# Weights of the third stage split by ScalarE and GpSimd and turned by DMA transposes; ScalarE makes the norms' shifts

## What is computed

```python
x = x + tanh(g_xattn[0]) * _L0_xattn_ref(_layernorm(x), ctx, ...)       # stage A
x = x + tanh(g_ffn[0])   * _L0_ffn_ref(_layernorm(x), w_fc, w_proj)     # stage B
x = x + tanh(g_xattn[1]) * _L1_xattn_ref(_layernorm(x), ctx, Wq, Wg, bg, Wkv, Wo)  # stage C
x = x + tanh(g_ffn[1])   * _L1_ffn_ref(_layernorm(x), ...)              # stage D

def bitlinear(x, w):                     # stage B, twice, with an exact gelu between
    xn = layer_norm(x)
    x_hat = xn + stop_gradient(absmax_quant(xn) - xn)   # clip at +-gamma * (128 - 1e-6) / 128
    w_hat = w + stop_gradient(ternarize_weights(w) - w) # sign * mean(abs(w))
    return einsum('bsd,od->bso', x_hat, w_hat)
```

## Time and profile before

| | |
|---|---|
| median of three runs | 1724.37 us (1722.57 to 1724.70) |
| profiled execution, first to last instruction | 1722.0 us |
| TensorE busy over the span | 1587.8 us (92%) |
| VectorE | 973.1 us (57%) |
| ScalarE | 709.2 us (41%) |
| GpSimd | 824.3 us (48%) |
| stage B in that execution | about 518.4 to 781.8 us |
| mean granted TensorE clock | 0.978 |

### The profile page before, as it was taken

The page is one execution under the profiler, slowest core; times in us unless marked ns, Lnnn a source line. Parts: engine busy times, 40 slices in busy tenths (PEclk is TensorE's granted clock), DMA queues, the critical chain, the costliest instruction groups (busy, mean ns, idle before and its releaser), DMA issues. The chain is left out here.

```text
span 1722.0 us, 29300 instructions
## 1 busy us (share of the span) xinstructions
PE 1587.8 (92%) x10826; PEld 829.3 (48%) x10826; DVE 973.1 (57%) x1947; ACT 709.2 (41%) x1311; POOL 824.3 (48%) x853
## 2 busy tenths in 40 slices
PE   5769999999877999899999989999999999999998
PEld 3336665665443444345656544444444444444443
DVE  5736666778736999845665543377454333211146
ACT  3268888888855655532232321211111111222221
POOL 3478887877853545443452434344333532112134
PEclk9989999999878999999999999999999999999999
DMA  6745444322333555444554426447454754477746
GB/s 182 160 102 112 99 106 109 93 67 72 92 73 84 110 119 114 93 86 86 96 120 95 78 74 156 110 105 153 92 101 101 154 101 95 109 173 172 168 138 195
DMA packets 453955, 195.68 MB, mean 114 GB/s; under 512 B 395500, under 2 KB 418286, under 8 KB 453816
## 3 DMA queue, kind: packets, MB, share of 16 engines
q1 hardware_dynamic: 448136, 175.19, 46.0%
q0 software_dynamic: 5680, 18.62, 4.1%
HBM read 77.17 MB, written 22.81 MB: 58 GB/s over the span
## 5 line engine op out<-in xcount | busy, mean ns | idle before, releaser
L1109 POOL TENSOR_TENSOR a_pl<-a_prob,a_ph 128x512 f16<-128x512 f32 x256 | 295.2, 1166 | 72.7 <-ACT a_prob L996 72.3
L1199 DVE TENSOR_REDUCE a_mx<-bank 128x2 f32<-128x512 f32 x256 | 173.3, 686 | 97.1 <-PE bank L690 95.5
L140 PE MATMUL bank<-XTh,d_whs 128*128 128x512 f16 x512 | 194.9, 381 | 4.2 <-PEq L89 2.4
L141 PE MATMUL bank<-XTl,d_whs 128*128 128x512 f16 x512 | 194.7, 380 | 0.0
L142 PE MATMUL bank<-XTh,d_wls 128*128 128x512 f16 x512 | 194.6, 380 | 0.0
L995 ACT ACTIVATE a_ph<-bank 128x512 f16<-128x512 f32 x256 | 153.9, 601 | 73.3 <-PE bank L710 35.9
L2384 POOL CAST d_cut<-d_raw 128x512 f16<-128x512 f32 x90 | 56.2, 624 | 227.7 <-DMA d_raw<-in_L_ffn_sw 146.8
L996 ACT ACTIVATE a_prob<-bank 128x512 f32<-128x512 f32 x256 | 154.4, 603 | 0.0
L2304 DVE TENSOR_TENSOR d_hid<-d_hid,bank 128x512 f32<-128x512 f32 x64 | 43.9, 686 | 172.1 <-PE bank L142 168.2
L2295 ACT ACTIVATE d_hid<-bank 128x512 f32<-128x512 f32 x64 | 38.2, 597 | 204.7 <-PE bank L142 204.7
L2299 ACT ACTIVATE d_hh<-d_hid 128x512 f16<-128x512 f32 x64 | 40.3, 630 | 194.7 <-DVE d_hid L2304 194.7
(11 more groups left out here) (349 smaller groups left out, 3996.4 us busy)
## 6 DMA issues: line engine op xcount, KB each, us to landing
d_raw<-in_L_ffn_w SPq DMA_DIRECT2D x48, 256.0 KB, 3.1
d_raw<-in_L_ffn_sw SPq DMA_DIRECT2D x42, 256.0 KB, 3.1
made<-e_y SPq DMA_DIRECT2D x39, 256.0 KB
a_stage<-in_L_ffn_w_fc SPq DMA_DIRECT2D x32, 256.0 KB, 2.9
a_stage<-in_L_ffn_w_proj SPq DMA_DIRECT2D x32, 256.0 KB, 3.1
a_fbuf<-in_ctx SPq DMA_DIRECT2D x16, 256.0 KB, 3.5
rows<-f_cut SPq DMA_DIRECT2D x16, 256.0 KB, 2.5
out_x<-X SPq DMA_DIRECT2D x16, 256.0 KB, 2.4
```

The source lines that it names most:

```text
L140: nc.tensor.matmul(out_ap, lhi, rhi, start=first, stop=False)
L141: nc.tensor.matmul(out_ap, lhi, rlo, start=False, stop=False)
L1109: nc.gpsimd.tensor_tensor(pl[:, n % NP, :], prob[:, n % 2, :], ph[:, n % NP, :], ALU.subtract).then_inc(ev["L"], 1)
L1199: nc.vector.tensor_reduce(mx[:, h, tt, half, 2 * (g % 4):2 * (g % 4) + 2], bank[BS + m % 2][:, :].rearrange("p (r k) -> p r k", r=2), AX_X ...
```

## The change

The norms' shifts are made by ScalarE: `front_norm` and `norm` each get two 128 x 1 operations (minus the mean; that times the power), each with a wait on the one before; VectorE's `front_mean` and `mean` are gone. A group of weights is now 128 rows of a matrix, loaded whole; ScalarE cuts the high part straight from the loaded rows into one of four buffers (`ccut`), GpSimd subtracts to get the low part, at the end of its iteration, and SyncE puts both in place with two DMA transposes per group, in iteration n those of groups 2n - 2 and 2n - 1, after `place_front`. A load waits for GpSimd's subtraction of three groups before, a high cut for the placing of four groups before. TensorE's transposes, PSUM banks 6 and 7 and VectorE's `low_weight` are not used for weights any more.

```diff
@@ phase_b: buffers @@
-    craw = sb("b_craw", [P, RG, 4, P])
+    fneg = sb("b_fneg", [P, LEAD, 2])
+    neg = sb("b_neg", [P, 2])
+    NG, RG, RC = 5 * KC, 3, 4
+    craw = sb("b_craw", [P, RG, D])
+    ccut = sb("b_ccut", [P, RC, 2, D], F16)
+    w_tp = [sem(f"w_turned{i}") for i in range(RC)]
@@ sync @@
             def load_weight(g):
                 if g >= RG:
-                    sp.wait_ge(w_tr, g - RG + 1)
-                w, k = group(g)
-                sp.dma_start(craw[:, g % RG], cw[w][:, k * P:(k + 1) * P].rearrange("(r p) c -> p r c", p=P))\
-                  .then_inc(w_in[g % RG], 16)
+                    sp.wait_ge(w_lo, g - RG + 1)
+                w, r = group(g)
+                sp.dma_start(craw[:, g % RG, :], cw[w][r * P:(r + 1) * P, :]).then_inc(w_in[g % RG], 16)
+
+            def place_weight(g):
+                w, r = group(g)
+                sp.wait_ge(w_lo, g + 1)
+                for low, home in enumerate((cwh, cwl)):
+                    sp.dma_start_transpose(home[:, w, :, r * P:(r + 1) * P], ccut[:, g % RC, low, :])\
+                      .then_inc(w_tp[g % RC], 16)
@@ sync, iteration n, after place_front(n + LEAD) @@
+                for g in (2 * n - 2, 2 * n - 1):
+                    if 0 <= g < NG:
+                        place_weight(g)
@@ tensor @@
-            def turn_weight(g):
-                pe.wait_ge(w_in[g % RG], 16 * (g // RG) + 16)
-                if g >= 2:
-                    pe.wait_ge(w_lo, g - 1)
-                for r in range(4):
-                    last = nc.tensor.transpose(bank[6 + g % 2][:, r * P:(r + 1) * P], craw[:, g % RG, r, :], ident[:, :])
-                last.then_inc(w_tr, 1)
@@ tensor, context @@
-                pe.wait_ge(w_lo, KC * (i + 1))
+                for t in range(RC):
+                    pe.wait_ge(w_tp[t], 32 * KC * (i + 1) // RC)
@@ scalar, front_norm; norm in the same way @@
-                act.wait_ge(f_nm, 2 * (f - LEAD) + v + 1)
+                act.wait_ge(f_var, 2 * (f - LEAD) + v + 1)
+                nc.scalar.activation(fneg[:, s, v:v + 1], fmv[:, s, 0:1], ACT.Copy, scale=-1.0).then_inc(f_nm, 1)
+                act.wait_ge(f_rs, 2 * (f - LEAD) + v + 1)
+                act.wait_ge(f_nm, 2 * (2 * (f - LEAD) + v) + 1)
+                nc.scalar.activation(frs[:, s, v, 1:2], fneg[:, s, v:v + 1], ACT.Copy,
+                                     scale=frs[:, s, v, 0:1]).then_inc(f_nm, 1)
+                act.wait_ge(f_nm, 2 * (2 * (f - LEAD) + v) + 2)
@@ scalar, high_weight @@
-                act.wait_ge(w_tr, g + 1)
-                nc.scalar.activation(cwh[:, w, k, :], bank[6 + g % 2][:, :], ACT.Copy).then_inc(w_hi, 1)
+                act.wait_ge(w_in[g % RG], 16 * (g // RG) + 16)
+                if g >= RC:
+                    act.wait_ge(w_tp[g % RC], 32 * (g // RC))
+                nc.scalar.activation(ccut[:, g % RC, 0, :], craw[:, g % RG, :], ACT.Copy).then_inc(w_hi, 1)
@@ gpsimd, called for groups 2n and 2n + 1 after front_cut(f) @@
+            def low_weight(g):
+                pool.wait_ge(w_hi, g + 1)
+                nc.gpsimd.tensor_tensor(ccut[:, g % RC, 1, :], craw[:, g % RG, :], ccut[:, g % RC, 0, :],
+                                        ALU.subtract).then_inc(w_lo, 1)
@@ vector: front_mean, mean, low_weight and their calls are removed @@
-                nc.vector.scalar_tensor_tensor(out=frs[:, s, v, 1:2], in0=fmv[:, s, 0:1], scalar=-1.0,
-                                               in1=frs[:, s, v, 0:1], op0=ALU.mult, op1=ALU.mult).then_inc(f_nm, 1)
...
-                nc.vector.tensor_tensor(cwl[:, w, k, :], bank[6 + g % 2][:, :], cwh[:, w, k, :],
-                                        ALU.subtract).then_inc(w_lo, 1)
```

More of the change, by code:

```diff
@@ L1400, in phase_b @@
     mhalf = sb("b_mh", [P, 1])
-    NG, RG = 5 * KC, 3
-    craw = sb("b_craw", [P, RG, 4, P])
+    fneg = sb("b_fneg", [P, LEAD, 2])
[3 more added lines that the diff above has]
+    ccut = sb("b_ccut", [P, RC, 2, D], F16)
     wkv = a["L1_xattn_Wkv"]
@@ L1406, in phase_b @@
     w_in = [sem(f"w_in{i}") for i in range(RG)]
-    w_tr, w_hi, w_lo = (sem("w_" + n) for n in ("tr", "hi", "lo"))
+    w_hi, w_lo = sem("w_hi"), sem("w_lo")
+    w_tp = [sem(f"w_turned{i}") for i in range(RC)]
     def group(g):
@@ L1478, in _ @@
                 sp.wait_ge(f_tp[i], 32 * (TILES // LEAD - 1))
+            for i in range(RC):
+                sp.wait_ge(w_tp[i], 32 * (NG // RC))
         @block.tensor
@@ L1529, in _ @@
                     up(n + 2)
-                for g in (2 * n, 2 * n + 1):
-                    if g < NG:
-                        turn_weight(g)
                 if n >= TILES - 2:
@@ L1556, in norm @@
             def norm(n):
-                act.wait_ge(b_nm, n + 1)
+                act.wait_ge(b_var, n + 1)
+                nc.scalar.activation(neg[:, n % 2:n % 2 + 1], mv[:, n % 2, 0:1], ACT.Copy, scale=-1.0).then_inc(b_nm, 1)
+                act.wait_ge(b_rs, n + 1)
+                act.wait_ge(b_nm, 2 * n + 1)
+                nc.scalar.activation(rs[:, n % 2, 1:2], neg[:, n % 2:n % 2 + 1], ACT.Copy,
+                                     scale=rs[:, n % 2, 0:1]).then_inc(b_nm, 1)
+                act.wait_ge(b_nm, 2 * n + 2)
                 nc.scalar.activation(h32[:, n % 2, :], h32[:, n % 2, :], ACT.Identity, bias=rs[:, n % 2, 1:2],
@@ L1658, in _ @@
                     front_cut(f)
+                for g in (2 * n, 2 * n + 1):
+                    if g < NG:
+                        low_weight(g)
                 if n == CNEXT:
@@ L1676, in front_moments @@
                                         ALU.add).then_inc(f_var, 1)
-            def front_mean(f, v):
-                s = f % LEAD
-                dve.wait_ge(f_rs, 2 * (f - LEAD) + v + 1)
-                nc.vector.scalar_tensor_tensor(out=frs[:, s, v, 1:2], in0=fmv[:, s, 0:1], scalar=-1.0,
-                                               in1=frs[:, s, v, 0:1], op0=ALU.mult, op1=ALU.mult).then_inc(f_nm, 1)
             def clip(x, q):
@@ L1705, in moments @@
                 nc.vector.tensor_scalar(ve[:, n % 2:n % 2 + 1], mv[:, n % 2, 1:2], 1e-6, None, ALU.add).then_inc(b_var, 1)
[L1707 to L1710, removed]
             def hidden_clip(n):
@@ L1719, in result @@
                                                in1=X[:, n, :], op0=ALU.mult, op1=ALU.add).then_inc(b_out, 1)
-            def low_weight(g):
-                w, k = group(g)
-                dve.wait_ge(w_hi, g + 1)
-                nc.vector.tensor_tensor(cwl[:, w, k, :], bank[6 + g % 2][:, :], cwh[:, w, k, :],
-                                        ALU.subtract).then_inc(w_lo, 1)
             for h in range(NH):
@@ L1729, in _ @@
             moments(0)
-            mean(0)
             stat(1, 0)
@@ L1735, in _ @@
             moments(1)
-            mean(1)
             for n in range(TILES):
@@ L1745, in _ @@
                     stat(m, 0)
-                if f < TILES:
-                    front_mean(f, 0)
                 if m < TILES:
@@ L1755, in _ @@
                     stat(m, 2)
-                if f < TILES:
-                    front_mean(f, 1)
                 if m < TILES:
@@ L1760, in _ @@
                     moments(m)
[L1761 to L1765, removed]
                 if f < TILES:
```

## The result

The changed kernel takes 1764.35 us (median of four runs, 1762.85 to 1766.99) beside 1723.47 for the kernel before in the same session: 1.0229 of it, interval 1.0215 to 1.0242. That is 40.9 us or 2.3% slower; 1764.2 was forecast. Its profiled execution spans 1760.8 us, 38.8 more than that of before; 1761.8 was forecast.

What follows compares the result with a forecast made beforehand. VectorE's loop, with ScalarE's normalisation, set the 15.7 us tile, SyncE's queue close behind at 14.3; 40 added transposes make the queue the bound at 19.6, the stage 39.8 us later: 1722.0 + 39.8 + 2.4 = 1764.2 us, range 1752 to 1774.

Steps and rivals of the forecast that it cites:

- The queue as the bound: SyncE's queue, iterations 1 to 10: 144 transposes and 15 loads fill it from 559.2 to 761.1 us, 19.6 per tile.
- The tail: From tile 12's hidden transposes on: nothing won back or lost, the feed-forward stage's end moves from about 780 to 820.
- the sum: SyncE's queue: 559.2 + 188.6 + 9.3 + 4.0 = 761.1, so iteration 11 starts 39.8 us later.
- VectorE: Feed-forward tile: it loses 4.1 us of shifts and weight subtractions, its loop falls from 15.7 to below 12 us.
- ScalarE's small operations: Six added 128x1 operations per tile at 0.2 us, 0.4 a pair; from above 1.10 each, from below the negation free.
- The new waits: T starts a tile's hidden transposes: second weight's low half ready at T + 8.6 to 9.5, wanted at T + 11.1.
- Rival B: Weight loads stall in SyncE's queue because transposes land late and shift pairs cost 2.2 us: + 8, 1772 us; chance 0.08.
- The clock: TensorE's slow matmuls after holes cost 2.5 us per tile, 16.4 in all, still below 19.6: no term.
- rival C: TensorE never regains its clock, matmuls stay at 0.42 us: + 67, 1831 us; chance 0.02.
- the price of the 40: Added weight transposes in SyncE's queue: 1.31 us each, from below 1.19, from above 1.31 and the occasional long one.

Runs made afterwards that it cites:

- e2: Changed kernel with the norms' shifts back on VectorE, so only the weights take the new way: 1769.1 us, 1.0262 of the kernel before.
- e4: Kernel before, nothing removed, plus 40 DMA transposes of a constant tile into scratch in SyncE's queue: 1766.8 us, 1.0242 of the kernel before.
- e3: Changed kernel with the 40 weight transposes made plain copies of the same blocks: 1738.47 us, 1.0083 of the kernel before.
- e6: Changed kernel without the 40 weight transposes, weight homes filled with a constant by GpSimd: 1711.61 us, 0.9919 of the kernel before.
- e1b: Second run of the kernel before with only the norms' shifts moved to ScalarE: 1709.35 us, 0.9907 of the kernel before.
- e1: Kernel before with only the norms' shifts moved to ScalarE, weights as before: 1713.22 us, 0.9931 of the kernel before.
- e7: Kernel before with the shifts on ScalarE and the context transposes moved to iterations 11 and 12: 1711.3 us, 0.9918 of the kernel before.
- e5: Kernel before with the shifts on ScalarE and the context transposes moved to iterations 12 and 13: 1717.17 us, 0.9957 of the kernel before.

## Why the prediction was right

**The queue as the bound.** Forecast: 144 transposes and 15 loads keep it without a gap for 201.9 us (188.6 + 9.3 + 4.0), from 559.2 to 761.1. The trace: 560.73 to 762.09, 201.4 us. It starts 1.5 us late: 0.9 because one of the long transposes (2.14 us, at 546.90) fell into iteration 0, for which I had counted none, and 0.55 because the transposes ahead of it already stood that much later than before (544.82 instead of 544.27). The pairs of loads cost 1.15 to the next start instead of 1.23, which takes back 0.6. The hidden transposes of the first nine tiles start 19.1 to 20.5 us apart, 19.75 on average, where 19.6 was forecast; TensorE waits 2.3 to 6.4 us ahead of the down projections of tiles 3 to 11, and 7.9 ahead of down 12, a wider spread than the 3 to 6 of the forecast. Undoing this part and doing it alone (e2, e4, e3, e6) leaves no other cause of size.

**The tail.** Down 12 starts 40.5 us later than before, and the stage ends 41.3 later (781.87 to 823.18): the forecast 39.8 is 1.5 short. 1.0 of it is there at the hidden transposes of tile 12 (762.09 for 761.1): the start was 1.5 late and the queue 0.5 quicker than its sum. Another 0.8 comes behind down 12, where the forecast let nothing be lost: from there to the end of the stage it takes 49.4 us instead of 48.7, for after the hole of 7.92 us twelve matmuls come 0.42 us apart, after the old one of 4.96 us eight. Down 12 itself takes 0.3 back, at 40.5 later. That the profiled span grew by 38.8 alone is no credit to the sum. The rest of the program took 940.1 us behind `c_bg` in the profile of before and 937.6 in that of the changed kernel, in code that is the same; over all ten profiles it took 936.6 to 942.1, and these two ends are one and the same kernel (e1b and e1). So 2.5 us of agreement or miss are within what executions differ by. The ratio of the medians, 40.9 us, is nearer to the stage's 41. So the sum was right to 1 or 2 us; that the forecast time of 1764.2 met the median of 1764.35 to 0.2 us is luck.

**VectorE.** 4.1 us per tile were to go; 14.5 - 10.9 = 3.6 went in the busy time. The operations taken out overlapped their neighbours, so that from their starts to the next ones they took 3.8, and the clip of the hidden tile became 0.2 longer (1.35 before, 1.56 at 608.76). The held 1.10 us operations are gone. That they were held until GpSimd's subtraction was through fits all three of a tile: they end at 608.91, 612.93 and 615.78, the subtractions at 608.90, 612.92 and 615.75 (timeline of GpSimd, kernel before, the last two):

```profile
611.76 1.16 POOL L1635 TENSOR_TENSOR b_hcut<-b_h,b_hcut 128x512 f16<-128x512 f32 x1
...
614.60 1.15 POOL L1635 TENSOR_TENSOR b_hcut<-b_h,b_hcut 128x512 f16<-128x512 f32 x1
```

e1 prices their removal: 13 to 16 us on the whole time, because VectorE's loop was the stage's period.

**ScalarE's small operations.** Timeline of ScalarE, changed kernel:

```profile
601.59 0.63 ACT L1590 ACTIVATE b_ccut<-b_craw 128x512 f16<-128x512 f32 x1 [0.99 <-DMA c_wl<-b_ccut]
602.13 0.19 ACT L1549 ACTIVATE b_fneg<-b_fmv 128x1 f32<-128x1 f32 x1
602.40 0.29 ACT L1552 ACTIVATE b_frs<-b_fneg,b_frs 128x1 f32<-128x1 f32 x1
602.73 0.81 ACT L1557 ACTIVATE f_x<-f_x,b_frs 128x512 f32<-128x512 f32 x1
```

A pair delays the normalisation by 0.60 us (602.13 to 602.73), where I took 0.4, between the two bounds and near the lower.

**The new waits.** With T = 600.41, the second weight cut waits for its slot's old transposes until T + 1.2 (forecast 1.1 to 2.0), and GpSimd's second subtraction ends here:

```profile
606.97 2.27 POOL L1652 TENSOR_TENSOR b_ccut<-b_craw,b_ccut 128x512 f16<-128x512 f32 x2
```

609.24 is T + 8.8 (forecast 8.6 to 9.5), and the loads stand at 610.83 without a gap in the queue. Rival B's stall did not come: the waits of ScalarE for the placing, 44.6 us in sum, were hidden whole.

**The clock.** The granted clock of the two tiles is 0.91 and 0.92, no step of the sum, as forecast: rival C is out. Up to 13 matmuls behind a hole came 0.42 us apart, which cost TensorE up to 2.7 us, inside time in which it would have waited for the queue; only behind down 12 did it count.

**What was right for a weaker reason.** I took the price of the 40 from the form of their destination and from the context transposes. The runs give a better one: the hidden transposes and e4's write four blocks side by side, the weights' four blocks that lie 512 columns apart, e4's come from another source, and the medians are 1.26 and 1.27 us. All move 128 x 512 f16; no run tried another size.

## What to carry to other kernels

The queue of an engine that computes nothing can be the bound, and no busy share shows it: add up its starts per tile, here 1.31 us for each transpose, before work is moved to DMA. Here transposes and loads took 14.3 of 15.7 us of the queue, so four more transposes (5.2 us) had to lengthen every tile, while relieving VectorE and TensorE could win nothing behind it. A change of two halves should be timed as halves: one won 13 to 16 us, the other lost 43. When a transfer is moved later, look up its first reader, not only the queue.

## What the runs showed that I had not expected

- Now and then a transpose holds the queue 1.4 to 2.7 us instead of 1.26, in every kernel (in the changed one at 546.90 with 2.14, 576.15 with 2.13, 614.52 with 1.90, 652.91 with 2.16, 692.62 with 2.08, 732.16 with 2.29, 775.20 with 2.24). The spacing is 29 us once and then 38 to 43 us there, and 23 to 30 us in the profile of e1. What sets it, no run here tells. Five of them lie between tile 2 and tile 12, 4.3 us over, where 4.0 were put into the sum.
- A hole's length does not alone decide TensorE's clock, nor is the first matmul behind it a sign of it. In the changed kernel seven matmuls behind a hole of 2.90 us (612.06) were at half the clock, at once. Behind 4.07 us (651.73) the first three came at full clock and the next eight at half. In e3 a hole of 1.97 us (659.49) was followed by two at full clock and eight at half. Behind this one of 3.34 us in the changed kernel none was slow:

```profile
691.46 0.39 PE L1517 MATMUL bank<-b_wpj,b_hTh 128*128 128x512 f16 x1 [3.34 <-DMA b_hTl<-b_hcut]
```

- The same small result is held by GpSimd's subtraction on VectorE and not on ScalarE: the 128x1 shift took 0.64 to 1.10 us on VectorE, and its last operation on ScalarE takes 0.29 to 0.30 us all 40 times, also where it runs during a subtraction (at 612.73, in one from 611.91 to 614.18).
- The same stages in the same code differ between executions by 4 us: the first up projection started at 521.7 to 522.8 us in seven of the ten profiles and at 526.0 to 526.3 in three, which a single span hides and the length of a stage doesn't. The three are e1, e1b and e7; e5, which differs from e7 only in a later part of SyncE's queue, is not among them. Why, no run tells.
